# A window-attention kernel with a software split of float32: squares and MLP input rounded from PSUM, one low half moved between engines, two orders rewritten

## The reference

```python
x = x + depthwise_conv31x31(group_norm(x), weight) + bias
x = x + window_block(group_norm(x))
```

```python
h = ln(t) ;  q, k, v = h @ wq + bq, h @ wk + bk, h @ wv + bv
t = t + softmax(q @ k.T / sqrt(8)) @ v @ wo + bo
h = ln(t) ;  t = t + gelu(h @ w1 + b1) @ w2 + b2
```

## Time and profile before

| what | value |
|---|---|
| median of 3 runs (lowest to highest) | 5947.31 us (5946.79 to 5955.28) |
| the profiled execution: its time, its span | 5965.81 us, 5964.0 us |
| granted TensorE clock over the span (1.00 is full) | 0.976 |
| PE busy | 5586.8 us (94%) |
| POOL, DVE, ACT busy | 3802.2 (64%), 3678.1 (62%), 3454.9 us (58%) |
| DMA | 740.86 MB, mean 124 GB/s |

### The profile page before, as it was taken

How to read it: one execution, slowest core, us unless ns; L and a number is a source line. 1 busy time by engine, 2 the same in 40 slices (tenths; PEclk the granted TensorE clock), 3 DMA queues, 4 the chain that set the end, 5 groups by cost and what they waited for, 6 DMA issues and landing times.

```text
span 5964.0 us, 233920 instructions
## 1 busy us (share of the span) xinstructions
PE 5586.8 (94%) x100144; PEld 4428.8 (74%) x100144; DVE 3678.1 (62%) x6074; ACT 3454.9 (58%) x4952; POOL 3802.2 (64%) x4822
## 2 busy tenths in 40 slices
PE   6999999999959999999999999999999999999998
PEld 6999999999946666666666666666666666666665
DVE  2222222222227777777777777777777777777774
ACT  3444444444336666666666666666666666666665
POOL 2222222222247888887878888888888888788875
PEclk9999999999959999999999999999999999999997
DMA  4444444444335666666666666666666666666662
GB/s 110 108 106 106 106 107 107 106 107 106 82 84 126 140 137 136 137 139 132 137 133 139 135 138 138 138 136 136 139 138 137 135 138 138 132 138 137 134 134 58
DMA packets 1099836, 740.86 MB, mean 124 GB/s; under 512 B 465429, under 2 KB 1070709, under 8 KB 1098709
## 3 DMA queue, kind: packets, MB, share of 16 engines
q1 hardware_dynamic: 1069620, 687.18, 51.8%
q0 software_dynamic: 29184, 38.71, 2.7%
HBM read 409.02 MB, written 316.46 MB: 122 GB/s over the span
## 4 chain that ended last, share of the span: by engine, by line
POOL 34%; issue 17%; PE 8%; DVE 7%; ACT 5%; POOLq 0%; DVEq 0%; ACTq 0%
POOL b_mid_hi L715 6%; POOL b_outs L780 5%; POOL b_mid_lo L722 5%; POOL b_sq_lo L761 4%; POOL b_t_lo L754 4%; POOL b_sq_lo L729 3%; POOL b_t L745 3%; DVE b_y L990 3%; ACT b_lg L802 3%; DVE b_h L975 2%; ACT b_rstd L807 2%; PE ps_ring L1037 2%; POOL b_t_hi L750 2%; DVE b_vd L983 1%; POOL b_mx_planes L789 1%
## 5 line engine op out<-in xcount | busy, mean ns | idle before, releaser
L223 POOL TENSOR_SCALAR xn<-xin,aff 96x896 f32<-96x896 f32 x192 | 233.9, 1218 | 1207.9 <-DVE aff L330 1195.2
L1092 PEld LDWEIGHTS ps_pv<-b_vd,b_probs_t 128*64 128x64 f32 x24576 | 772.5, 140 | 163.8 <-issue 154.8
L908 DVE TENSOR_REDUCE b_mx<-ps_s 113x12 f32<-113x588 f32 x1024 | 783.4, 765 | 174.7 <-PE ps_s L1046 173.9
L815 ACT ACTIVATE b_probs_t<-ps_t 128x588 f32<-128x588 f32 x1024 | 666.9, 651 | 332.1 <-PE ps_t L1046 306.4
L417 PE MATMUL ps_conv<-toep_hi,blocks_hi 128*128 128x304 f32 (+5 forms) x4032 | 844.2, 291 | 0.0
L417 PE MATMUL ps_conv<-toep_hi,blocks_lo 128*128 128x304 f32 (+5 forms) x4032 | 839.1, 290 | 0.0
L417 PE MATMUL ps_conv<-toep_lo,blocks_hi 128*128 128x304 f32 (+5 forms) x4032 | 838.0, 289 | 0.0
L1092 PE MATMUL ps_pv<-b_vd,b_probs_t 128*64 128x18 f32 x24576 | 824.0, 213 | 0.4 <-issue 0.3
L722 POOL TENSOR_TENSOR b_mid_lo<-b_mid,b_mid_hi 128x392 fp32r<-128x392 f32 x768 | 789.8, 1028 | 22.0
L353 DVE SCALAR_TENSOR_TENSOR x1t<-ps_conv,biasb,xin 128x896 f32<-128x896 f32 x96 | 110.5, 1151 | 1024.4 <-PE ps_conv L417 1024.4
L780 POOL TENSOR_TENSOR b_outs<-b_y,b_xs 96x392 f32<-96x392 f32 x256 | 317.7, 1241 | 524.8 <-DVE b_y L990 524.8
(11 more groups left out here) (145 smaller groups left out, 12574.1 us busy)
## 6 DMA issues: line engine op xcount, KB each, us to landing
stacked_qk<-b_planes SPq DMA_DIRECT2D x512, 220.5 KB, 2.9
b_q_st<-stacked_qk SPq DMA_DIRECT2D x512, 220.5 KB, 4.4
b_k_st<-stacked_qk SPq DMA_DIRECT2D x512, 220.5 KB, 5.7
toep<-filters_padded SPq DMA_DIRECT2D x96, 936.5 KB, 6.9
stacked_qk<-b_planes SPq DMA_DIRECT2D x512, 147.0 KB, 2.3
stacked_qk<-b_planes SPq DMA_DIRECT2D x512, 73.5 KB, 1.9
b_xs<-x_scratch SPq DMA_DIRECT2D x224, 147.0 KB, 2.8
out<-b_outs SPq DMA_DIRECT2D x224, 147.0 KB, 3.2
```

What stands on the lines that cost most here:

```text
L815: act.activation(pt[:, p, 0:HEADS * TOK].rearrange("k (e n) -> k e n", e=2), ps_t[:, :, 0:HPAIR * TOK], ACT.Exp, scale=float(DH) ** -0.5). ...
L908: dve.tensor_reduce(mx[0:rows_q, :].rearrange("q (e m p) -> q e m p", e=2, p=PAIRS)[:, :, :, p], ps_s[0:rows_q, :, 0:HPAIR * TOK].rearrang ...
L1092: ins = pe.matmul(to, pt[:, p, at:at + WS], vd[:, m % VR, p, h, :, :], start=True, stop=True, skip_group_check=True)
```

## The change

Six things change, all in `window_pass`:

- `sq1_hi` and `sq2_hi` are no longer rounded from `sq1` and `sq2` by DVE. ACT does the square twice, from PSUM, once into the rounded tile and once into the plain one.
- `h2_hi` is no longer rounded from `h2` by DVE: DVE does the scaling twice, from PSUM, the rounded tile first.
- `sq2_lo` is formed by DVE in place of POOL.
- plane 1 of the row maxima is rounded by POOL in place of DVE.
- POOL's order: `mid_high(0)` stands behind the copy of the wrapped columns, `mid_high(1)` right behind `mid_low(0)`.
- PE's order: `below_max(2)` stands ahead of the third `expand` in place of behind the transposes of `o`.

```diff
                 gn, qkv, att, proj, mlps = (strip(i, s, x) for x in (GN, QKV, ATT, PROJ, MLPS))
                 if qkv is not None:
                     pool.wait_ge(S["sq1_high"], qkv + 1)
+                    pool.wait_ge(S["sq1"], qkv + 1)
                     pool.tensor_tensor(sq1_lo[:, :], sq1[:, :], sq1_hi[:, :].bitcast(F32), ALU.subtract).then_inc(
                         S["sq1_split"], 1)
-                mid_high(mlps, 0, i)
                 if gn is not None:
                     slg, img = gn % B, gn // B
                     if slg == 0:
@@ -738,7 +738,9 @@
                         pool.wait_ge(S["gn_col"], img + 1)
                     pool.wait_ge(x_loaded[gn % XS], x_landed(gn))
                     pool.tensor_copy(xs[:, gn % XS, :, HW:XW], xs[:, gn % XS, :, 0:SHIFT]).then_inc(S["wrapped"], 1)
+                mid_high(mlps, 0, i)
                 mid_low(mlps, 0)
+                mid_high(mlps, 1, i)
                 if gn is not None:
                     pool.wait_ge(S["wrapped"], gn + 1)
                     after(pool, i, "t1_done", gn - B + 1)
@@ -753,13 +755,8 @@
                     pool.wait_ge(S["t0_high"], gn + 1)
                     pool.tensor_tensor(t0_lo[:, gn % 2, :], t0[:, gn % B, :], t0_hi[:, gn % 2, :].bitcast(F32),
                                        ALU.subtract).then_inc(S["t0_split"], 1)
-                mid_high(mlps, 1, i)
                 mid_low(mlps, 1)
                 mid_high(mlps, 2, i)
-                if proj is not None:
-                    pool.wait_ge(S["sq2_high"], proj + 1)
-                    pool.tensor_tensor(sq2_lo[:, :], sq2[:, :], sq2_hi[:, :].bitcast(F32), ALU.subtract).then_inc(
-                        S["sq2_split"], 1)
                 mid_low(mlps, 2)
                 if qkv is not None:
                     pool.wait_ge(S["q_done"], qkv + 1)
@@ -779,6 +776,10 @@
                         pool.wait_ge(stored[sl % 2], 16 * before)
                     pool.tensor_tensor(tokens(outs[:, sl % 2]), windows(y[:, sl % 2, :]), tokens(xs[:, mlps % XS]),
                                        ALU.add).then_inc(S["added"], 1)
+                if att is not None:
+                    pool.wait_ge(S["mx_rest"], att + 1)
+                    pool.tensor_scalar(mx_planes[:, 1, :, :], mx_rest[:, :, :], 1.0, 0.0, ALU.mult, ALU.add).then_inc(
+                        S["mx_mid"], 1)
                 if mlps is not None:
                     sl = mlps % B
                     pool.wait_ge(S["added"], mlps + 1)
@@ -815,9 +816,11 @@
                 act.activation(pt[:, p, 0:HEADS * TOK].rearrange("k (e n) -> k e n", e=2),
                                ps_t[:, :, 0:HPAIR * TOK], ACT.Exp, scale=float(DH) ** -0.5).then_inc(S["exp_done"], 1)
 
-            def square(i, n, dst, src, done, split, scale=1.0):
+            def square(i, n, dst, src, done, split, scale=1.0, used=None):
                 act.wait_ge(S[src], n + 1)
                 after(act, i, split, n)
+                if used:
+                    after(act, i, used, n)
                 act.activation(dst[:, :], ps_xc[0:C, 0:NT], ACT.Square, scale=scale).then_inc(S[done], 1)
 
             def gelu(i, s, n, m, use):
@@ -832,6 +835,8 @@
                 qkv, soft, proj, mlps = (strip(i, s, x) for x in (QKV, SOFT, PROJ, MLPS))
                 exps(i, soft, 0)
                 if qkv is not None:
+                    square(i, qkv, sq1_hi, "xc1", "sq1_high", "sq1_split", 1.0 / C, "var1")
+                if qkv is not None:
                     square(i, qkv, sq1, "xc1", "sq1", "sq1_split", 1.0 / C)
                 exps(i, soft, 1)
                 act.preload_act_table_set("gelu_apprx_tanh_and_others")
@@ -843,10 +848,13 @@
                     log_var(qkv, bank(i, s, "var1"), "var1", "lg1")
                 if qkv is not None:
                     after(act, i, "h2_done", qkv - (PROJ - QKV))
+                    after(act, i, "h2_high", qkv - (PROJ - QKV))
                     inv_std(qkv, "lg1", "rstd1")
                 exps(i, soft, 2)
                 if proj is not None:
                     square(i, proj, sq2, "xc2", "sq2", "sq2_split")
+                if proj is not None:
+                    square(i, proj, sq2_hi, "xc2", "sq2_high", "sq2_split", used="var2")
                 if qkv is not None:
                     act.wait_ge(S["q_ps"], qkv + 1)
                     if qkv > 0:
@@ -909,17 +917,10 @@
                                   ps_s[0:rows_q, :, 0:HPAIR * TOK].rearrange("q e (m t) -> q e m t", m=HPAIR), AX.X,
                                   ALU.max).then_inc(S["mx_done"], 1)
 
-            def high(i, n, dst, src, ready, used, per, done):
-                dve.wait_ge(S[ready], n + 1)
-                after(dve, i, used, per * n)
-                dve.tensor_copy(dst[:, :], src[:, :]).then_inc(S[done], 1)
-
             def step(i, s):
                 qkv, att, proj, mlps = (strip(i, s, x) for x in (QKV, ATT, PROJ, MLPS))
                 pv = ps_pv[:, 0:PAIRS * HEADS * VA].rearrange("q (n d) -> q n d", d=VA)
                 row_max(i, att, 0)
-                if qkv is not None:
-                    high(i, qkv, sq1_hi, sq1, "sq1", "var1", 1, "sq1_high")
                 if proj is not None:
                     dve.wait_ge(S["pv_ps"], 2 * (proj + 1))
                     dve.reciprocal(rden[:, :].unsqueeze(2), pv[:, :, DH:VA]).then_inc(S["rden_done"], 1)
@@ -948,7 +949,10 @@
                                              ALU.mult).then_inc(S["h1_done"], 1)
                 row_max(i, att, 3)
                 if proj is not None:
-                    high(i, proj, sq2_hi, sq2, "sq2", "var2", 1, "sq2_high")
+                    dve.wait_ge(S["sq2_high"], proj + 1)
+                    dve.wait_ge(S["sq2"], proj + 1)
+                    dve.tensor_tensor(sq2_lo[:, :], sq2[:, :], sq2_hi[:, :].bitcast(F32), ALU.subtract).then_inc(
+                        S["sq2_split"], 1)
                 if qkv is not None:
                     dve.wait_ge(S["q_high"], qkv + 1)
                     after(dve, i, "qk_split", qkv)
@@ -971,10 +975,13 @@
                         S["mx_rest"], 1)
                 if proj is not None:
                     dve.wait_ge(S["rstd2"], proj + 1)
+                    after(dve, i, "w1_ps", NM * proj)
+                    after(dve, i, "h2_split", proj)
+                    dve.tensor_tensor(h2_hi[:, :], ps_xc[0:C, 0:NT], rstd[:, :], ALU.mult).then_inc(S["h2_high"], 1)
+                if proj is not None:
+                    dve.wait_ge(S["rstd2"], proj + 1)
                     after(dve, i, "h2_split", proj)
                     dve.tensor_tensor(h2[:, :], ps_xc[0:C, 0:NT], rstd[:, :], ALU.mult).then_inc(S["h2_done"], 1)
-                if proj is not None:
-                    high(i, proj, h2_hi, h2, "h2_done", "w1_ps", NM, "h2_high")
                 if qkv is not None:
                     dve.wait_ge(S["v_ps"], qkv + 1)
                     after(dve, i, "pv_ps", 2 * (qkv - VR + 1))
@@ -991,11 +998,9 @@
                                              t1[:, mlps % 2, :], ALU.add, ALU.add).then_inc(S["y_done"], 1)
                 if proj is not None:
                     dve.wait_ge(S["h2_high"], proj + 1)
+                    dve.wait_ge(S["h2_done"], proj + 1)
                     dve.tensor_tensor(h2_lo[:, :], h2[:, :], h2_hi[:, :].bitcast(F32), ALU.subtract).then_inc(
                         S["h2_split"], 1)
-                if att is not None:
-                    dve.wait_ge(S["mx_rest"], att + 1)
-                    dve.tensor_copy(mx_planes[:, 1, :, :], mx_rest[:, :, :]).then_inc(S["mx_mid"], 1)
             steps(dve, step)
 
         @block.tensor
@@ -1099,6 +1104,7 @@
                 if qkv is not None:
                     pe.wait_ge(S["t0_split"], qkv + 1)
                     after(pe, i, "h2_done", qkv - (PROJ - QKV))
+                    after(pe, i, "h2_high", qkv - (PROJ - QKV))
 
                     pe.matmul(ps_xc[0:C, 0:NT], centre[:, :], t0_hi[:, qkv % 2, :], start=True, stop=False)
                     pe.matmul(ps_xc[0:C, 0:NT], centre[:, :], t0_lo[:, qkv % 2, :], start=False,
@@ -1109,6 +1115,7 @@
                 expand(i, s, mlps, 0, "w1a")
                 expand(i, s, mlps, 1, "w1b")
                 scores(i, att, 1)
+                below_max(i, soft, 2)
                 expand(i, s, mlps, 2, "w1c")
                 if proj is not None:
                     pe.wait_ge(S["o_done"], proj + 1)
@@ -1117,7 +1124,6 @@
                     for n in range(PAIRS):
                         ins = pe.transpose(turned[:, n // 2, :, n % 2, :], o[:, n, :], cc("ident"))
                     ins.then_inc(S["ot_ps"], 1)
-                below_max(i, soft, 2)
                 scores(i, att, 2)
                 if qkv is not None:
                     spread(i, s, qkv, "var1", sq1_hi, sq1_lo, "sq1_split", "var1")
```

## The result

The changed kernel takes 5901.44 us in the median of 5 runs (5877.03 to 5913.35), the one before 5954.18 us in 5 runs (5946.79 to 5955.28). The ratio is 0.991, 95% interval 0.9881 to 0.9939: 0.9% faster. The forecast was 5857 us, its range 5745 to 5910; the median lies inside it. The profiled execution took 5913.35 us against 5965.81, 52 us less where 90 was forecast.

What follows compares the result with a forecast made beforehand. A chain through several engines, closing once a step with PE waiting at `var2` for POOL's sq2_lo, bounds the window pass. Period 16.11 to 15.75 us, 0.36 less in 249 steps: 5947.31 - 90 = 5857 us, range 5745 to 5910.

Steps and rivals of the forecast that it cites:

- h2 from PSUM: Window pass, DVE: the cast goes, a second 0.56 us product comes; `y` and `outs` 0.83 us earlier.
- V: Window pass, PE: start of `var2`, the sum over sq2; zero point of the forecast's times within a step.
- POOL: Run from `outs` to the third mid_lo's end: 11.54 us falls to 10.15 (-0.98, -0.53, +0.12).
- ACT: Two more squares, 0.43 us of occupation each; h1 still ends at 12.3, as the third gelu hangs on PE.
- X: Window pass, PE: start of `xc2`, the second centring; forecast at 12.32 us into the step, 12.81 before.
- PE's order: `below_max(2)` moved on PE fills the time in which the third `expand` waited for its bank; cost 0.
- sq2_lo on DVE: DVE's subtraction meets POOL's third mid_lo, waits for it and ends at 15.25 us, not 14.78.
- DVE gets in ahead: Case in which DVE's sq2_lo starts before POOL's mid_lo and so isn't held; no chance of its own.
- the first rival: DVE's sq2_lo doesn't wait for POOL, or precedes mid_lo: period about 15.33, 194 us gained, 5753 us; chance 0.17.
- The last leg: From POOL's third mid_lo's end through DVE's sq2_lo and q's remainder to PE's next `var2`: 0.91 us.
- V': Start of the next step's `var2` on PE; forecast 15.75 us behind the last one, against 16.11 before.
- The second: Rival: the wait for POOL's mid_lo returns the whole gain or more, at worst 5967 us; no gain 0.06, slower 0.10.

Runs made afterwards that it cites:

- the pair with and without the wait: Changed kernel with POOL's t0_lo moved behind the third mid_lo: with POOL also waiting there for sq2_lo 5818.6 us, without that wait 5870.85 us.

## Why the prediction was right, and where its size was off

Point by point, with the numbers of the step shown above:

- *h2 from PSUM.* `outs` forecast at V+4.69, measured 4.65. Alone on the kernel before it gave 161 us; without it the rest is 51 us slower than before, and no different over the steps at full clock. The part is right, and it carries the whole gain. What I took from the rows of `outs` without remark is the other side of the same exclusion: it takes 1.24 us in the median of 256, before and changed, and 0.97 at the end of the pass, where no h2_lo runs beside it. h2_lo starts just ahead of it and holds it for 0.27 us in each step. As it does so in both kernels, the forecast isn't touched.
- *POOL.* Its run from `outs` to the end of the third mid_lo was forecast at 10.15 us and is 10.12 (4009.06 to 4019.18). The rounding of the plane, which the old trace lacked, takes 0.27 us there, inside the bounds, and lengthens the run by 0.13 where I had 0.12; the wait ahead of sq1_lo is gone.
- *ACT.* h1 ends at V+12.32 (4016.73), as forecast (12.3). X is at V+12.47 and not 12.32, since PE's own work fills the time until then (with PE's old order it is V+12.27); PE waits 0.68 us later all the same, so nothing hangs on it. ACT's busy time grew by 0.55 us and not by the 0.86 that I reckoned, as the two more squares partly fill short gaps.
- *PE's order.* Forecast at 0; measured at 0.2 us on the way to X and 0 in the step.
- *sq2_lo on DVE.* Forecast to end 0.41 behind mid_lo, measured 0.43. That the meeting costs what it does is shown by the pair with and without the wait, and by putting the instruction back on POOL, not only by the row.
- *The evidence was misread, to no harm.* I wrote that in the convolution pass the meeting occurs once. toep_lo falls inside a running L223 of POOL with 32x448 elements 31 times, and in 30 of them it goes the other way: POOL's instruction starts 0.11 to 0.13 us ahead, and yet toep_lo takes 2.11 us and POOL's is held, 2.67 us in place of 0.73. The one that I used had a lead of 0.15. I wrote that these rows agree with the rule that the later one waits; by the starts of the profile that one row does and the other 30 don't. One of the 30, with toep_lo at 132.91:

```profile
132.78 2.67 POOL L223 TENSOR_SCALAR xn<-xin,aff 32x448 f32<-32x448 f32 x1
```

So the start that the profile shows doesn't tell who is first when the two are 0.1 us apart; in the window pass a lead of 0.05 to 0.12 us was enough for POOL's mid_lo (sq2_lo at 1.33 to 1.40 in the kernel with the cast restored). The forecast didn't hang on it, since mid_lo's lead was reckoned at 0.43 and is 0.55. But "DVE gets in ahead", part of the first rival, had more for it than my account gave.
- *The last leg was too short.* From mid_lo's end to V' I reckoned 0.91 us and it is 1.05. The missing 0.14 is behind q's remainder: it ends at 4020.08 and PE starts at 4020.23, 0.15 later, where I had put 0.02 to 0.04, after the gap behind sq2_lo before the change. This is the term that was mis-sized. Why it is longer isn't shown: that it is a PSUM bank that comes free isn't enough, since PE starts 0.06 us behind DVE's row maxima, which free one too. The two also differ in which of PE's two waits at `var2` ends last. All in all that makes 0.07 us a step with the other small differences: 15.82 in place of 15.75, some 17 us in all.
- *Clock.* I carried the time over at the same granted clock. The profiled executions had 0.976 and 0.971. With 4.2 to 4.4 us for each 0.001 that is 21 us, and 249 x 0.29 - 21 = 51, close to the 52 measured between the two profiles. The traces say the same: between 1850 and 5700 us a stretch of lower clock touches 4 steps before and 9 changed, most of 20 to 22 us. Over all runs whose clock is on record the two kernels overlap (before 0.968 to 0.980, changed 0.969 to 0.979), so it isn't shown that the change lowers the clock.
- *The basis.* The 5947.31 us from which I subtracted came from three runs; 5 gave 5954.18, 7 on another occasion 5964.56. At equal clock the gain is 78 us, against the 90 forecast.

The first rival (no exclusion, step 15.33) has fallen: DVE's subtraction is free only when POOL is idle or comes later. The second (given back, or more) didn't come about, but its rule holds: with the cast restored, V is at 4190.39, mid_lo ends at 4205.57, that is V+15.18, all but the place from which I had said that nothing is gained, and V' is at 4206.61; the step, 16.22, is above the old 16.11 by what the last leg was too short.

So the sign and the mechanism were right, and of the 90 us forecast the two profiled executions show 52. What I had not seen is the comparison that mattered most: by my own sum, h2's part alone was worth more than the whole change. I priced each part inside the full set and never asked for the best subset.

## What to carry to other kernels

Before an elementwise step is moved between DVE and POOL, look at what the other engine does at that very moment, not at busy shares: the move took 1.0 us from POOL and cost 0.4 us a step (15.82 against 15.43). A result that is to be rounded is cheapest rounded from PSUM, twice if need be. Where DVE and POOL meet on the path that closes the loop, a wait that keeps the one with time to spare out can pay, and so can a small delay that lets the other come first. A set of edits should be costed one by one and by subsets.

## What the runs showed of the hardware

- The exclusion, in one number: a DVE cast or two-tile subtraction that is held by a running POOL instruction ends behind it by its own time less 0.14 us: 0.42 to 0.43 us if it takes 0.56 alone, 0.22 if it takes 0.36 alone. In the 233 meetings of sq2_lo in the changed kernel the median is 0.42. The further POOL has got, the less is lost: sq2_lo takes 1.40 us behind a lead of 0.05 us, 1.10 behind 0.34, 0.89 behind 0.56 and 0.79 behind 0.65, over the kernels here. Held the other way, POOL's mid_lo ends 0.88 us behind sq2_lo's end, its 1.02 less 0.14.
- A DVE product or subtraction with one side in PSUM isn't held: h2_hi takes 0.56 us beside POOL's L768 (4005.82 to 4007.52).
- The kernel with the cast restored, in which PE stood idle 1.1 us at `var2` in most steps, had a granted clock a little below full over most of the pass. From 4100 to 4120 us it is 1.00, and then:

```profile
4120.00:4140.00 20.00, 18.77 (x410) 13.71 (x409) 13.67 (x23) 12.59 (x22) 15.07 (x21) 0.91 0.68 146
```

The slices of 20 us from 4140 to 4200 us are at 1.00 again: short stretches at the lower of the two levels (1.2 and 2.4 GHz). The kernels with 0.3 to 0.7 us of idle time there show 1.00 in most windows and fall in a few: 3 to 9 steps in each, and 13 in the kernel with PE's order back, which is idle 0.87 us, against 54. Whether the longer idle time is the cause was not tested.
